# Image blur moved behind the mix: mix in two parts, raw images placed one by one

## What is computed

```python
low_part = jnp.sum(xu * lf, axis=3).reshape(N, C, H, W)
out_low = (low_part * (inside_all + 1.0) - inside_all * gap) * lamb_l[None, :, None, None]
x = out_low + x * (lamb_h[None, :, None, None] + 1.0)
x_ht = dht_2d(x)
out_ht = out_ht.at[:, :, :M1, :M2].set(compl_mul2d(x_ht[:, :, :M1, :M2], w1))
y = dht_2d(out_ht) / (H * W)
y = gaussian_smoothing_4d(y)      # radius 4, axis 0 is the 8 images
return y * mask
```

## Time and profile before

| | us |
|---|---|
| median of 3 runs | 155.11 (154.5 to 155.58) |
| profiled execution | 156.23 |
| its span | 154.3 |
| PE busy | 132.8 |
| DVE busy | 62.0 |
| ACT busy | 36.4 |
| POOL busy | 39.4 |
| DMA, share of the 16 engines for SP's queue | 72.8% |

### The profile page before, as it was taken

How to read it: one execution, slowest core, us unless ns; L and a number is a source line. 1 busy time by engine, 2 the same in 40 slices (tenths; PEclk the granted TensorE clock), 3 DMA queues, 4 the chain that set the end, 5 groups by cost and what they waited for, 6 DMA issues and landing times.

```text
span 154.3 us, 5759 instructions
## 1 busy us (share of the span) xinstructions
PE 132.8 (86%) x2574; PEld 80.7 (52%) x2574; DVE 62.0 (40%) x127; ACT 36.4 (24%) x85; POOL 39.4 (26%) x21
## 2 busy tenths in 40 slices
PE   6967468999999799999797699999999999999600
PEld 5523222545454445455565688677585775755200
DVE  1033850464646354546139312243434433344400
ACT  3000410111111011111218412433333333332300
POOL 8999000314645180917520000000000000000000
PEclk9999996999999999999999999999999999999995
DMA  4999999999999996000000000069999999999997
GB/s 113 351 359 269 370 351 348 363 378 362 382 350 362 350 350 207 0 4 4 0 4 2 4 4 0 6 206 330 314 340 302 340 309 325 337 314 338 345 340 237
DMA packets 34438, 37.31 MB, mean 242 GB/s; under 512 B 800, under 2 KB 33824, under 8 KB 34416
## 3 DMA queue, kind: packets, MB, share of 16 engines
q1 hardware_dynamic: 34272, 36.90, 72.8%
q10 hardware_dynamic: 144, 0.07, 0.4%
HBM read 20.19 MB, written 16.78 MB: 240 GB/s over the span
## 4 chain that ended last, share of the span: by engine, by line
PE 73%; DMA 8%; SPq 6%; ACT 3%; issue 2%; DVE 1%; DVEq 0%
PE ps L559 19%; PE ps L373 15%; DMA x_ring<-x 8%; PE ps L538 8%; PE ps L517 6%; PE ps L390 6%; PE ps L361 3%; PE ps L495 3%; ACT mixin L615 3%; PE ps L426 3%; PE ps L413 3%; PE ps L445 2%; SPq L315 2%; SPq L322 2%; SPq L325 2%
## 5 line engine op out<-in xcount | busy, mean ns | idle before, releaser
L373 PE MATMUL ps<-x_ring,k_wide 64*64 64x512 f32 x256 | 32.6, 626 | 6.0 <-DMA x_ring<-x 6.0
L718 DVE STREAM_TRANSPOSE y_sb<-ps 128x1024 f32<-128x1024 f32 x16 | 20.0, 1250 | 33.0 <-PE ps L373 33.0
L559 PE MATMUL ps<-cols,k_wide 128*64 128x330 f32 (+1 forms) x192 | 30.2, 464 | 0.0
L559 PEld LDWEIGHTS ps<-cols,k_wide 128*64 128x64 f32 x192 | 13.2, 136 | 12.7 <-issue 4.7
L373 PEld LDWEIGHTS ps<-x_ring,k_wide 64*64 64x64 f32 x256 | 8.5, 137 | 20.6 <-issue 12.9
L590 DVE COPY rows<-ps 128x330 f32<-128x330 f32 (+1 forms) x24 | 12.6, 525 | 13.3 <-PE ps L559 12.7
L871 POOL TENSOR_TENSOR spread<-parts,k_wide 128x960 f32<-128x960 f32 (+2 forms) x6 | 10.1, 1688 | 23.6 <-ACT parts L642 23.6
L361 PE MATMUL ps<-idle 128*128 128x256 f32 x46 | 14.3, 463 | 1.2 <-DVE idle L709 1.2
L590 ACT COPY rows<-ps 128x330 f32<-128x330 f32 (+1 forms) x24 | 11.1, 462 | 17.7 <-PE ps L559 16.6
L390 PE MATMUL ps<-y_sb,k_wide 64*64 64x96 f32 x512 | 14.2, 248 | 0.0
L538 PEld LDWEIGHTS ps<-k_wide,modes 64*64 64x64 f32 x384 | 11.8, 134 | 3.9 <-issue 3.9
(11 more groups left out here) (60 smaller groups left out, 98.5 us busy)
## 6 DMA issues: line engine op xcount, KB each, us to landing
x_ring<-x SPq DMA_DIRECT2D x16, 1024.0 KB, 11.4
out<-rows SPq DMA_DIRECT2D x16, 640.0 KB, 4.9
out<-rows SPq DMA_DIRECT2D x8, 768.0 KB, 6.4
w_sb<-mix_w SPq DMA_DIRECT2D x2, 960.0 KB, 12.2
k_wide<-wide SPq DMA_DIRECT2D x1, 528.0 KB, 12.5
k_tab<-narrow SPq DMA_DIRECT2D x1, 361.2 KB, 10.5
k_wide<-wide SPq DMA_DIRECT2D x1, 321.0 KB, 12.0
k_wide<-wide SPq DMA_DIRECT2D x1, 128.0 KB, 5.6
```

Of the source, the lines that this page charges most:

```text
L373: last = nc.tensor.matmul(ps[64 * t:64 * t + 64, 2 * g + e, :], k_wide[rows_in, O_LT + 64 * r:O_LT + 64 * r + 64], x_ring[rows_in, u, 8 * ...
L559: last = nc.tensor.matmul(ps[64 * g:64 * g + 64, B_F[k % 3], 0:nt * NW], const(O_LH + s * H + r * H // 2, (1, H // 2)), cols[:, u, 6 * g:6 ...
L718: nc.vector.transpose(view(y_sb[:, g, 0, 0, 0:1], (1, 1024)), view(ps[:, 2 * g, 0:1], (1, 1024))).then_inc(y_out, 1)
```

## The change

The blur over images moves behind the mix. `parts` of each image (now with the negated plane, a second ScalarE operation) are placed straight into `mixin`, by POOL for images 0 to 6, four copies each, and by ScalarE and DVE, two copies each, for image 7. The mix has two passes: images 0 to 5 (48 columns a matmul, in two halves of 10 columns b, around the coefficients of image 7) and images 6 and 7 (16 columns a matmul), right behind turn 0. The unmixed result goes to a new tile `raw`, and DVE makes `mixed` of image n out of it in as many steps as the matrix has entries in its row, each 96 x 160 and each waiting for the one before (`blur_step`). A turn waits for its image's steps. The weights and last tables are loaded behind all of x. The fillers behind the start are gone, PSUM banks are dealt out anew, and the zeroing of PSUM gaps comes before the last columns are turned. For images 0 and 1 the order of the write stage changes; from image 2 on DVE's loop is written out.

```diff
@@ constants and tiles @@
-O_BT = O_RU + 4 * 64
-O_L = O_BT + N * N
+O_L = O_RU + 4 * 64
...
+    EARLY = 6
+    PASS = (EARLY, N - EARLY)
+    HB = MODES // 2
+    weight = blur_matrix(N)
+    blurred_at = np.cumsum(np.count_nonzero(weight, axis=1)).tolist()
...
-        parts = sb("parts", [128, 2, 2, HALFP])
-        spread = sb("spread", [128, N, PLANE])
-        acc = sb("acc", [128, N, PLANE])
+        parts = sb("parts", [128, 2, 3, HALFP])
...
-        mixin = sb("mixin", [128, HALFP, J, 3, N])
+        mixin = [sb(f"mixin{i}", [128, HALFP, J, 3, size]) for i, size in enumerate(PASS)]
+        raw = sb("raw", [Q * C, N, S * J, MODES])
...
-        B_T, B_F = 3, (5, 6, 7)
-        B_TURN, B_MIX = 1, 5
+        B_T, B_F = 4, (0, 1, 6)
+        B_TURN, B_MIX = 2, (0, 7)
@@ sync @@
             for n in range(3, N):
                 for g in range(2):
                     load(n, g)
-                if n < 5:
-                    cut = slice((n - 3) * part, (n - 2) * part)
-                    sp.dma_start(w_sb[:, cut, :], mix_w[:, cut, :]).then_inc(weights_in[n - 3], 16)
-                if n == 5:
-                    sp.dma_start(k_wide[:, O_TW:], wide[:, O_TW:]).then_inc(rest_in, 16)
+            for i in range(2):
+                cut = slice(i * part, (i + 1) * part)
+                sp.dma_start(w_sb[:, cut, :], mix_w[:, cut, :]).then_inc(weights_in[i], 16)
+            sp.dma_start(k_wide[:, O_TW:], wide[:, O_TW:]).then_inc(rest_in, 16)
@@ tensor: the fillers behind image 7 and the single mix go @@
+            def mix(i, half):
+
+                size, at = PASS[i], 2 * J * PASS[i]
+                for b in range(half * HB, half * HB + HB):
+                    bank, slot = (b // HB, b % HB) if i == 0 else (0, b)
+                    for q in range(Q):
+                        for s in range(S):
+                            last = nc.tensor.matmul(
+                                view(ps[q * C:(q + 1) * C, B_MIX[i] + bank, slot * at:slot * at + 1], (1, at)),
+                                w_sb[:, (s * Q + q) * MODES + b, :],
+                                mixin[i][:, q * MODES + b, :, 1 - s:3 - s, :], start=(s == 0), stop=(s == 1))
+                last.then_inc(mix_done, 1)
...
             def turn(n):
 
-                if from_(n, 1):
+                pe.wait_ge(blur_step, blurred_at[n])
+                if n == 0:
+                    pe.wait_ge(rest_in, 16)
+                    pe.wait_ge(gaps_zero, 1)
+                else:
...
+            for half in weights_in:
+                pe.wait_ge(half, 16)
+            pe.wait_ge(y_out, 2 * N - 1)
+            pe.wait_ge(placed, EARLY)
+            stage2(N - 1, 1)
+            edge_sums(N - 2)
+            mode_sums(N - 2)
+            logits(N - 1)
+            mix(0, 0)
+            coefficients(N - 1)
+            mix(0, 1)
+            edge_sums(N - 1)
+            mode_sums(N - 1)
             turn(0)
-            keep_busy(2)
+            pe.wait_ge(placed, N - 1)
+            pe.wait_ge(placed_act, 1)
+            pe.wait_ge(placed_dve, 1)
+            mix(1, 0)
+            mix(1, 1)
             await_modes(0)
             to_columns(0, 0)
             turn(1)
-            for n in range(N):
-                to_rows(n, n % 2, 0, next_columns=n + 1 < N)
+            to_rows(0, 0, 0)
+            await_modes(1)
+            to_columns(1, 1)
+            to_rows(0, 0, 1)
+            to_rows(1, 1, 0)
+            turn(2)
+            to_rows(1, 1, 1)
+            await_modes(2)
+            to_columns(2, 0)
+            turn(3)
+            for n in range(2, N):
+                to_rows(n, n % 2, 0)
                 if n + 1 < N:
+                    await_modes(n + 1)
                     to_columns(n + 1, (n + 1) % 2)
@@ scalar @@
                 nc.scalar.copy(view(parts[:, n % 2, 0, 0:1], (1, PLANE)),
-                               ps[:, B_SMALL, AT_SUM:AT_SUM + PLANE]).then_inc(parts_done, 1)
+                               ps[:, B_SMALL, AT_SUM:AT_SUM + PLANE])
+                nc.scalar.mul(parts[:, n % 2, 2, :], ps[:, B_SMALL, AT_SUM:AT_SUM + HALFP],
+                              -1.0).then_inc(parts_done, 1)
...
+            act.wait_ge(mix_done, 1)
+            unmix(nc.scalar.copy, 0, 0, 0, HB)
+            unmix(nc.scalar.copy, 0, 1, 0, 1)
+            unmix(nc.scalar.copy, 0, 1, 1, HB - 1).then_inc(raw_act, 1)
+            keep_basis(N - 1)
+            keep_parts(N - 1)
+            act.wait_ge(parts_done, N)
+            place_parts(nc.scalar.copy, N - 1, 0)
+            place_parts(nc.scalar.copy, N - 1, 1).then_inc(placed_act, 1)
@@ vector @@
+            def blur(n, images):
+
+                for k in images:
+                    share = float(weight[n, k])
+                    if share == 0:
+                        continue
+                    to, of = mixed[:, n, :, 0:MODES], raw[:, k, :, :]
+                    if k == max(n - REACH, 0):
+                        last = nc.vector.tensor_scalar(to, of, share, None, ALU.mult)
+                    else:
+                        dve.wait_ge(blur_step, steps[0])
+                        last = nc.vector.scalar_tensor_tensor(to, of, share, to, op0=ALU.mult, op1=ALU.add)
+                    steps[0] += 1
+                    last.then_inc(blur_step, 1)
...
+            dve.wait_ge(mix_done, 2)
+            unmix(nc.vector.tensor_copy, 0, 0, HB, HB)
+            unmix(nc.vector.tensor_copy, 0, 1, HB, HB).then_inc(raw_dve, 1)
...
+            early, late = range(EARLY), range(EARLY, N)
+            blur(0, early)
+            dve.wait_ge(parts_done, N)
+            place_parts(nc.vector.tensor_copy, N - 1, 2)
+            place_parts(nc.vector.tensor_copy, N - 1, 3).then_inc(placed_dve, 1)
             modes_step(0, 0)
+            blur(1, early)
             cols_step(0, 0)
             modes_step(1, 1)
...
+            for n in range(2, N):
+                rows_step(n, n % 2, n // 2, (1,))
+                if n + 1 < N:
+                    cols_step(n + 1, (n + 1) % 2)
+                if n + 2 < N:
+                    modes_step(n + 2, n % 2)
+                rows_step(n, n % 2, n // 2, (3,))
+                if n + 3 < N:
+                    blur(n + 3, range(N))
+                rows_step(n, n % 2, n // 2, (5,))
@@ gpsimd @@
-            for n in range(N - 1):
-                spread_step(n)
+                for j in range(J):
+                    last = place_parts(nc.gpsimd.tensor_copy, n, j)
+                last.then_inc(placed, 1)
```

More of the change, by code:

```diff
@@ L200, in constants @@
     wide[:, O_LT:O_RU] = lt
-    wide[:, O_RU:O_BT] = ru
-    wide[:, O_BT:O_L] = blur_matrix(N).T.reshape(1, -1)
+    wide[:, O_RU:O_L] = ru
     wide[:, O_L:O_EYE] = lsum
@@ L654, in _ @@
                 filters(n)
-            keep_basis(N - 1)
-            keep_parts(N - 1)
-            act.wait_ge(last_share, 1)
-            act.wait_ge(zeroed, 2)
-            for j in range(J):
-                last = place_minus_odd(j)
-            last.then_inc(mixin_act, 1)
-            act.wait_ge(mix_done, 1)
-            unmix(nc.scalar.copy, 0)
-            act.wait_ge(mix_done, 3)
-            unmix(nc.scalar.copy, 2).then_inc(mixed_act, 1)
             def modes_step(n, u):
@@ L695, in _ @@
             modes_step(1, 1)
-            for n in (0, 1):
-                write_step(n, n, 0)
+            rows_step(0, 0, 0, (0, 2))
+            cols_step(1, 1)
+            rows_step(0, 0, 0, (4,))
+            rows_step(1, 1, 0, (0, 2))
+            modes_step(2, 0)
+            rows_step(1, 1, 0, (4,))
+            cols_step(2, 0)
+            modes_step(3, 1)
             with act.Fori(1, N // 2 - 1) as it:
@@ L789, in _ @@
                 products(n - 1)
-            turn_columns(N - 1)
-            products(N - 1)
-            dve.wait_ge(acc_done, N - 1)
-            dve.wait_ge(parts_done, N)
-            share = blur_matrix(N)[:, N - 1]
-            for k in np.flatnonzero(share):
-                last = nc.vector.scalar_tensor_tensor(
-                    acc[:, int(k), :], view(parts[:, 1, 0, 0:1], (1, PLANE)), float(share[k]), acc[:, int(k), :],
-                    op0=ALU.mult, op1=ALU.add)
-            last.then_inc(last_share, 1)
-            dve.wait_ge(last_share, 1)
-            dve.wait_ge(zeroed, 2)
-            for j in range(J):
-                last = place_parts(nc.vector.tensor_copy, j)
-            last.then_inc(mixin_dve, 1)
-            for quad in range(4):
-                bank, slot = (1, NF - 1 - LOWER) if quad % 2 == 0 else (0, 0)
-                last = nc.vector.memset(ps[32 * quad:32 * quad + 32, B_TURN + bank, slot * C:slot * C + C], 0.0)
-            last.then_inc(gaps_zero, 1)
-            dve.wait_ge(mix_done, 2)
-            unmix(nc.vector.tensor_copy, 1).then_inc(mixed_dve, 1)
+            steps = [0]
+            def blur(n, images):
[11 more added lines that the diff above has]
+                    last.then_inc(blur_step, 1)
             def modes_step(n, u):
```

(29 more changed lines are left out.)

105 lines of the change are left out of this document (26 added, 79 removed).

## The result

The changed kernel took 159.08 us (median of 4 runs, 157.56 to 159.87), the kernel before on the same chips 155.35 (4 runs, 154.5 to 156.01): ratio 1.023, with an interval of 1.014 to 1.032. It is slower by 2.3%, where 1.8% faster was forecast. The profiled execution took 158.97 us, its span is 157.0. Executions of one kernel differ by some per cent with the granted clock, and the ratios leave the disturbed ones out, so a ratio can differ a little from that of two medians.

The account below looks back on a forecast made before the run. TensorE's pace bounds the write stage, store queue nearly full; the change works in the seam (72 to 97 us). 6.3 - 1.2 - 2.4 = 2.7, 2.8 with roundings; 155.11 - 2.8 = 152.3 us, range 149.3 to 155.5.

Parts of the forecast that it names:

- (2): Mix in two passes: 16.6 ns a record, so 2.0 us for each half of the first, 4.0 for the second.
- (6): Second mix pass behind turn 0, 84.0 to 88.0; columns of image 0 at 88.0, 6.3 us earlier.
- mix(1) over 4.7: Sign of being wrong: the second mix pass, put at 4.0 us, takes more than 4.7.
- a granted clock under 1 between 72 and 97: Sign of being wrong: TensorE's clock falls between the end of the eight images and the writing.
- The rival of a floor: Mix: small matmuls have a least time each; 153.7 us at 19.6 ns, 156.3 at 25 ns; chance 0.10.
- the clock falls without fillers: Rival: six us of work partly at 1.2 in place of 2.4 GHz, 3.9 us more, 156.2; chance 0.07.
- Stalls in images 2 to 4: Write stage: blur steps between the copies of chunks 3 and 5 make TensorE wait 1.2, 0.9, 0.5; 2.4 with overlap.
- Rows of image 0 to rows of image 2: Early write stage: blur steps in DVE's queue delay TensorE, costing 1.2 us of the 6.3 gained.
- Blur pitch: DVE's dependent blur steps of 96x160 start 0.35 us apart, bounds 0.24 and 0.50; called the deciding step.
- Turn 0: Behind the blur of image 0: starts at 82.75, takes 1.24 us, over at 84.0.
- Parts copies 0.22 more: Each parts copy gets a negated copy of 60 columns behind it, 0.22 us, bounds 0.13 and 0.26.
- Placing on ScalarE 0.5 each: Image 7's placing beside turn 0: two ScalarE copies, bounds 0.26 and 1.09, 0.8 each before it shows.

Follow-up runs that it names:

- Experiment 8: The kernel of experiment 7 with the blur of images 5 to 7 between the copies of chunks 3 and 5: 157.91 us, ratio 1.017 to the kernel before.
- experiment 5: The changed kernel with the weights and last tables loaded amid the images, as before: 158.94 us, ratio 1.020 to the kernel before.
- experiment 9: The kernel of experiment 7 with fillers back around the coefficients of image 7 and the blur of image 2 earlier: 152.28 us, ratio 0.978 to the kernel before.
- experiment 1: The changed kernel with the second mix pass cut to half its matmuls (s=1 left out): 153.84 us, ratio 0.989 to the kernel before.
- experiment 7: The changed kernel with one mix pass of 64 columns ahead of turn 0, few fillers, blur behind chunk 5: 156.53 us, ratio 1.001 to the kernel before.
- experiment 6: The changed kernel with the blur of images 5 to 7 behind the copy of chunk 5 instead of between chunks 3 and 5: 158.87 us.
- experiment 2: The changed kernel with 64 columns in place of 16 in each second-pass matmul, same number of instructions: 158.85 us, ratio 1.023 to the kernel before.

## Why the prediction was wrong

The step that failed is (2), the price of the mix's records, above all where it stands in (6): "mix(1) 4.0", from a price per record between 13.6 and 19.6 ns. As a price it was even too high: within a block a record of 16 columns took 13 ns (124 in 1.57 us), and one of 48 columns 15.7 (117 in 1.84). What it lacked is a price per *block of instructions*: mix(1) took 84.49 to 90.75, 6.26 us, because it reaches into three blocks, whose starts stand 3.0 and 3.45 us apart (83.70, 86.67, 90.12). The bounds came from rows of 16 and 238 records, both shorter than two blocks and with fillers or waits ahead, so that the supply could catch up; neither could show a limit that is only reached when several blocks are run through at full pace. Two of the signs that the prediction had named for being wrong came true with it: mix(1) over 4.7, and a granted clock under 1 between 72 and 97 (0.84 from 86). The rule of the Trainium skill that I set beside it (TensorE: Matmul & The Clock Gate, "Wait — 56ns, not 53.3ns?", about 25 ns between matmuls) came out nearly right as an average here, 6.26/240 = 26 ns, and wrong as told for single ones, which ran 13 ns apart. That the average agrees is a coincidence: it is made of two stops and not of a spacing. The rival of a floor (0.10) had the right place, the mix, by that same luck.

Term by term, against the forecast on the profiled execution's basis (156.23 - 2.8 = 153.4; measured 158.97, so 5.5 more):

- *Supply gaps in the seam, forecast 0*: 0.83 in mix(0), 1.03 and 1.88 in mix(1). Part of it is given back by records cheaper than forecast: mix(1) is 2.3 over its 4.0, both halves of mix(0) 0.7 over. Columns of image 0: 90.77 against 88.0, 2.8 late.
- *Half clock behind the gap, forecast 0*: 1.15 (2.70 for 1.55). The rival "the clock falls without fillers" had the right mechanism at another place: not a wait for an engine, a wait for instructions.
- *Gap in turn 4, forecast 0*: 2.1. The border of a block stands there, and its packet came late; no other part of the change touches the matmuls of turn 4.
- *Stalls in images 2 to 4, forecast 2.4*: 2.2 (from the start of columns 3 to columns 7 30.25 us against 25.99, less the 2.1): 1.07, 0.72 and 0.38 where 1.2, 0.9 and 0.5 were forecast. Experiment 8 gives 1.9 to 2.4. Right in size, place and cause.
- *Rows of image 0 to rows of image 2, forecast 1.2*: 0.8. Near, 0.4 too dear. With the 2.8, 1.15, 2.1 and -0.2 above this makes 5.4 of the 5.5.
- *Blur pitch, forecast 0.35*: 0.355 (mean 321 ns, x44). Right; this was called the deciding step and was not. The prediction let the rule of the Trainium skill (VectorE: DVE Perf Modes, The DRAIN you can't avoid), that a semaphore after each operation costs nothing extra, stand for its lower bound of 0.24, "some 3 us more"; taken as no time beyond the 0.32 of the step itself it is 0.03 on 33 steps, 1 us. No run leaves the semaphores out, so what they cost is not shown.
- *Turn 0, forecast 82.75*: 83.18, with the gap of 0.83 in front of it, partly hidden. *Parts copies 0.22 more*: 0.13 (82.31 to 82.70). *Placing on ScalarE 0.5 each*: 0.63, hidden. *POOL's copies 0.42 each*: 0.52, so four took 2.13 and were over at 71.07, ahead of 71.86. *Weights*: nothing, by experiment 5.
- *"One gap called issue ... could go; bounds 0 and 1.13; I take 0"*: it grew to 2.09. At 72 us both kernels were level all the same (stage 2 at 71.86 and 71.85), so it is not in the sum. That is luck: the changed kernel began 0.50 earlier and without the half clock of the first half of stage 1 (1.95 in place of 3.23), and lost as much by the longer gap and half clock behind it (3.36 in place of 1.88). This gap was the hint: it is a supply gap, and it stood in the rows of the prediction without a cause.

The 0.83, 1.03, 1.88, 1.15 and 2.1 are 7.0 us. My estimate, with each of them counted in full, is that the changed kernel would have taken 152.0 without them. That the plan itself was sound is shown by experiment 9, which keeps the blur behind the mix without the second pass, has the fillers back, and takes 152.28. What the two passes cost was paid for in instructions: 449 more in all.

**Left open.** Why the packet for turn 4 started only at 112.61, 4.8 us behind the start of the block before it (107.84), where those of the seam started 0.7 to 1.5 behind theirs, is only argued. In the changed kernel the delay is 0.4 to 1.5 us from 62 to 97, where next to no other transfers run, and 1.8 to 5.0 in the stage of x loads up to 57 and in that of the stores (a share of 0.83), so the packet may queue behind them. But in the kernel before it is at times 0.5 under stores too, and no run took the stores away. The gap at record 722 follows the same delay: it is 2.09 us where the packet started 4.9 behind (changed kernel), 1.13 at 3.9 (before), and absent at 3.0 (experiment 1). It stands in experiments 7 and 9 alike and was followed by half clock only in 7; why is not shown. The time of experiment 6 is inconclusive.

## What to carry to other kernels

Count the instructions between two points, not only their time: 240 added records cost 6.6 us, large matmuls with about as much work 2.3 (experiments 3 and 4). A stretch called issue, amid the records of one line, that stands a multiple of 128 records from the next one and ends behind a packet of the instruction queue, was the instruction supply here; merge small matmuls, or spread them among waits that are there anyway. Long chains of dependent steps belong behind the last copy that a bank waits for, and fillers around short cross-engine chains stay until a run without them shows that the clock holds.

## What the runs showed of the hardware

- TensorE's instructions come in packets of 16,384 bytes: 256 instructions, 128 records and their weight loads (gaps 256, 513 and 1024 instructions apart). Where blocks were run through at full pace, their starts stood 2.97 and then 3.45 us apart, in experiment 2 and in the changed kernel alike, the second 27 ns a record, while within a block they ran 13 ns apart.
- A packet took 0.9 to 1.2 us on its queue in front of these gaps, and TensorE went on 1.26 to 1.51 us behind its landing.
- Work ahead of such a gap is free (experiment 2: 1.9 us more work, the same time).
- The granted clock fell to 1.2 GHz in or behind gaps of 1.9 and 2.1 us (at 88.24 and 49.49 of the changed kernel), but also behind two waits of 0.6 and 0.8 us that came close together (experiment 7, half clock from 77.45 to 84.27). It did not fall behind a gap of 1.86 (turn 4 of the changed kernel), nor behind one of 2.09 in experiment 9.
- A dependent VectorE step of 160 columns: 0.321 us, 0.355 from one start to the next.
